# Two more VectorE instructions per rounding step in a two-layer macaron transformer on eight cores

## The reference

```python
x = x + 0.5 * ffn(layernorm(x), w1, conv_w, conv_b, w2)   # L0, call f0a
x = x + attn(layernorm(x))                                # L0
x = x + 0.5 * ffn(layernorm(x), ...)                      # L0, call f0b
x = x + 0.5 * ffn(layernorm(x), ...)                      # L1, call f1a
x = x + attn(layernorm(x))                                # L1
x = x + 0.5 * ffn(layernorm(x), ...)                      # L1, call f1b

def act_quant(x):
    scale = 127.0 / clip(max(abs(x), axis=-1), 1e-5)
    return clip(round(x * scale), -128, 127) / scale
def bit_linear(x, w):      # values of the forward pass
    return act_quant(x) @ weight_quant(w).T
def ffn(x, w1, conv_w, conv_b, w2):
    h = silu(depthwise_conv1d(bit_linear(x, w1), conv_w, conv_b))
    return bit_linear(h, w2)
```

## Time and profile before

| | us |
|---|---|
| median of the 2 runs shown | 11792.54 |
| fastest and slowest of them | 11703.24, 11881.84 |
| the profiled execution | 11800.77 |
| its span, from the first instruction of core 4 to the last | 11799.2 |
| spans of the 8 cores in it | 11674.3 to 11799.2 |

### The profile page before, as it was taken

One profiled execution on the slowest core, in us unless ns is written; L12 is line 12 of the kernel. 1 busy time (PEld: TensorE's weight loads), 2 busy tenths in 40 slices (PEclk: granted clock), 3 DMA queues, 4 the chain that ended last, 5 costly groups with the idle time before them and its releaser, 6 DMA issues.

```text
span 11799.2 us, 83085 instructions; the slowest of 8 cores (11674.3 to 11799.2 us)
## 1 busy us (share of the span) xinstructions
PE 8035.5 (68%) x27412; PEld 4436.9 (38%) x27412; DVE 4650.7 (39%) x5551; ACT 2367.6 (20%) x4432; POOL 1504.8 (13%) x1037
## 2 busy tenths in 40 slices
PE   0165768777899999846573155757799999883656
PEld 0022223232677677422221022223476777531222
DVE  4687741111111110148776587740101111017965
ACT  0221022222333333012100122021333333102200
POOL 0022510000000000002252012520000000000244
PEclk9677767776555555767776577868655555586877
DMA  6322210000000000001235412310000000000232
GB/s 219 109 80 96 74 36 27 32 32 27 29 11 11 22 11 1 15 14 79 96 75 181 140 64 97 75 42 26 24 4 8 4 4 4 15 14 25 96 94 85
DMA packets 134609, 619.99 MB, mean 53 GB/s; under 512 B 17193, under 2 KB 17737, under 8 KB 102250
## 3 DMA queue, kind: packets, MB, share of 16 engines
q1 hardware_dynamic: 70378, 253.67, 7.0%
q0 software_dynamic: 39616, 176.45, 4.6%
q10 hardware_dynamic: 24192, 184.56, 3.8%
HBM read 403.19 MB, written 209.85 MB: 52 GB/s over the span
## 4 chain that ended last, share of the span: by engine, by line
PE 49%; DVE 26%; DMA 10%; issue 6%; ACT 5%; POOL 2%; DVEq 1%; ACTq 0%; POOLq 0%; SPq 0%
PE pmLL L1420 7%; PE psS0L L1212 6%; PE psC0L L1198 5%; PE pmW L1328 4%; PE psC2L L1198 4%; PE psS2L L1212 4%; PE psC3L L1198 4%; PE psC1L L1198 4%; PE pmL1b L1647 1%; PE pmL1a L1583 1%; ACT L1230 1%; DVE sAf1a L666 1%; DMA g_wq<-wslP 1%; DVE sAf0a L666 1%; DVE sAf0b L666 1%
## 5 line engine op out<-in xcount | busy, mean ns | idle before, releaser
L1243 DVE TENSOR_TENSOR pr00L<-pr00L,maskt 128x128 f32<-128x128 f32 x128 | 37.4, 293 | 2825.0 <-ACT pr10L L1230 2825.0
L1328 PE MATMUL pmW<-woS,ctT 128*128 128x512 f32 x1024 | 523.9, 671 | 126.6 <-DVE ctT L1313 72.0
L411 ACT ACT_TABLE_LOAD x6 | 7.7, 1283 | 2959.9 <-DMA g_wq<-wslP 1260.4
L1230 ACT ACTIVATE pr00L<-psS0L,stats 128x256 f32<-128x256 f32 x576 | 272.5, 473 | 1034.9 <-PE psS1L L1212 1033.4
L1230 ACT ACTIVATE pr01L<-psS2L,stats 128x256 f32<-128x256 f32 x576 | 272.5, 473 | 1004.6 <-PE psS3L L1212 992.2
L725 POOL TENSOR_TENSOR zsq0f1b<-sZ0f1b 128x2048 f32<-128x2048 f32 x16 | 57.6, 3599 | 3159.0 <-DVE sAf1b L666 3013.4
L712 ACT ACT_TABLE_LOAD x124 | 159.1, 1283 | 1293.8 <-DVE sZ0f1b L694 167.0
L1420 PE MATMUL pmLL<-xlnT,wp0L 128*128 128x512 f32 x768 | 413.4, 710 | 7.6 <-DMA wp0L<-wq 7.6
L1420 PE MATMUL pmLL<-xlnT,wp1L 128*128 128x512 f32 x768 | 416.9, 715 | 0.0
L725 POOL TENSOR_TENSOR zsq0f0b<-sZ0f0b 128x2048 f32<-128x2048 f32 x16 | 57.6, 3599 | 2583.6 <-DVE sAf0b L666 2441.0
L1328 PEld LDWEIGHTS pmW<-woS,ctT 128*128 128x128 f32 x1024 | 214.9, 216 | 414.7 <-issue 414.7
(11 more groups left out here) (698 smaller groups left out, 20509.4 us busy)
## 6 DMA issues: line engine op xcount, KB each, us to landing
wbA<-w1t SPq DMA_DIRECT2D x8, 2048.0 KB
wbB<-w1t POOLq DMA_DIRECT2D x8, 2048.0 KB, 11.5
g_silu<-sZ0f0a ACTq DMA_DIRECT2D x16, 1024.0 KB, 3.9
g_silu<-sZ1f0a ACTq DMA_DIRECT2D x16, 1024.0 KB, 3.9
g_silu<-sZ0f0b ACTq DMA_DIRECT2D x16, 1024.0 KB, 4.0
g_silu<-sZ1f0b ACTq DMA_DIRECT2D x16, 1024.0 KB, 3.9
g_silu<-sZ0f1a ACTq DMA_DIRECT2D x16, 1024.0 KB, 4.0
g_silu<-sZ1f1a ACTq DMA_DIRECT2D x16, 1024.0 KB, 3.9
```

The costliest lines, as they stand in the source:

```text
L1230: T.inc(se.activation(pr[hd][v % 2][:], psS[2 * (v % 2) + hd][:, 0:256], AF.Exp, bias=stats[:, NEGM:NEGM + 1], scale=0.125), "se")
L1328: te.matmul(pm[:, nb * 512:(nb + 1) * 512], ctT[:, c * P:(c + 1) * P], woS[:, c * D + nb * 512:c * D + (nb + 1) * 512], start=(c == 0), st ...
```

## The change

In both roundings the constant ahead of the conversion to integer is lowered by 1, and the fraction left over, which then can be up to one larger, is compared with 2.0 as well as with 1.0; the two comparison results are added. In `vq` and in `vqb` this is one more comparison (a TENSOR_SCALAR, 128 x 1024 float32) into a new tile, and one more sum (a SCALAR_TENSOR_TENSOR, 128 x 1024 float32). The new comparison stands ahead of the old one. In `vqb` the tick `e_tick` stays on the old comparison. Each call gets two new SBUF tiles of 4 KB per partition, `xt2` (stage 2) and `e1b` (stage 4).

```diff
+RB2 = -1.0009765625
@@ vq, for each of 16 token tiles
-                        T.inc(ve.tensor_single_scalar(r0x[:], xt1[:], RB, ALU.add), "ve")
+                        T.inc(ve.tensor_single_scalar(r0x[:], xt1[:], RB2, ALU.add),
+                              "ve")
                         T.sw(ve, "ve")
                         T.inc(ve.tensor_tensor(xt0[:], xt1[:], r0x[:], ALU.subtract),
                               "ve")
                         T.sw(ve, "ve")
+                        T.inc(ve.tensor_single_scalar(xt2[:], xt0[:], 2.0, ALU.is_ge),
+                              "ve")
+                        T.sw(ve, "ve")
                         T.inc(ve.tensor_single_scalar(xt0[:], xt0[:], 1.0, ALU.is_ge),
                               "ve")
+                        T.sw(ve, "ve")
+                        T.inc(ve.scalar_tensor_tensor(xt0[:], xt2[:], 1.0, xt0[:],
+                                                      ALU.mult, ALU.add), "ve")
                         T.sw(ve, "ve")
@@ vqb, for each of 64 iterations
-                    T.inc(ve.tensor_single_scalar(r0b[:], Ub[:], 128.4990234375,
+                    T.inc(ve.tensor_single_scalar(r0b[:], Ub[:], 127.4990234375,
                                                   ALU.add), "ve")
                     T.sw(ve, "ve")
                     T.inc(ve.scalar_tensor_tensor(
                         buf[:], Ub[:], 128.5, r0b[:], ALU.add, ALU.subtract), "ve")
                     T.sw(ve, "ve")
+                    T.inc(ve.tensor_single_scalar(
+                        e1b[:], buf[:], 2.0, ALU.is_ge), "ve")
+                    T.sw(ve, "ve")
                     e_tick = T.inc(ve.tensor_single_scalar(
                         Ub[:], buf[:], 1.0, ALU.is_ge), "ve")
+                    T.sw(ve, "ve")
+                    T.inc(ve.scalar_tensor_tensor(
+                        Ub[:], e1b[:], 1.0, Ub[:], ALU.mult, ALU.add), "ve")
                     T.sw(ve, "ve")
```

More of the change, by code:

```diff
@@ L481, in ffn_call @@
                 xt1 = a0.enter_context(nc.sbuf_tensor(f"xt1{tag}", [P, D], F32))
+                xt2 = a0.enter_context(nc.sbuf_tensor(f"xt2{tag}", [P, D], F32))
                 r0x = a0.enter_context(nc.sbuf_tensor(f"r0x{tag}", [P, D], I32))
@@ L899, in ffn_call @@
                 r0b = b1.enter_context(nc.sbuf_tensor(f"r0b{tag}", [P, 1024], I32))
+                e1b = b1.enter_context(nc.sbuf_tensor(f"e1b{tag}", [P, 1024], F32))
                 qsl = [b1.enter_context(nc.sbuf_tensor(f"qsl{j}{tag}", [P, 1024], BF16))
```

## The result

| | before | after |
|---|---|---|
| median | 11854.59 us (10 runs) | 12444.99 us (11 runs) |
| lowest, highest | 11703.24, 11913.13 | 12342.35, 12503.44 |
| profiled execution | 11800.77 | 12413.86 |
| spans of its cores | 11674.3 to 11799.2 | 12246.3 to 12412.3 |

The change makes the kernel slower: ratio 1.0524, 95% interval 1.0467 to 1.0581, 590 us between the medians. The forecast was 12348 us with a range of 12120 to 12560. In some executions one die runs at a lower granted clock and takes longer; the ratios and their intervals leave those out, and the rows of e5 and e6, whose profiled executions were of this kind, are from a core of the other die.

What follows compares the result with a forecast made beforehand. The prediction took VectorE's serial chain to bound the input rounding and a loop through GpSimd's loads and products the second matmul; 136 + 411 = 547 us on the profiled 11800.8 gave 12348 us, range 12120 to 12560.

Steps and rivals of the forecast that it cites:

- Input rounding: Input rounding: two new VectorE instructions add 2.13 us per tile, covered by nothing; 16 tiles x 4 calls, 136 us.
- Second matmul: Second matmul: plain pairs of iterations grow by 3.52 us, block ends by less; 25.7 us per block, 16 blocks, 411 us.
- The loop load, comparison, product as the limit of before: Second matmul before: comparison, GpSimd's load issues, wait and product close on the pair's 12.75 us; VectorE idles 2.59.
- VectorE sets the pace after the change: Second matmul: VectorE's own 12.79 us per pair uses up its idle time; with stretches the pair becomes 16.26 us.
- Both pairs of products now cost VectorE time: Second matmul: without VectorE idle time, both pairs of GpSimd's products stretch its instructions, together 3.48 us per pair of iterations.
- The price of the odd products: Second matmul: GpSimd's products of odd iterations stretch VectorE's instructions by the usual 1.74 us; bounds nothing to 2.73.
- full blocking: Second matmul: one pair of products per pair of iterations costs VectorE 2.73, +120 us, 12468; both 12590; chance 0.17.
- the main case: Whole kernel: the summed growth of 547 us holds, time 12270 to 12420 us; chance 0.60.
- The ends of blocks: Second matmul: the first pair behind the correction grows by 2.5 us, the pair with the correction by 2.1.
- The rival that ended on the other side: Second matmul: VectorE displaces GpSimd undisturbed, so the stage barely grows; 11950 us, +1.3%, not slower by 2%; chance 0.05.
- The Trainium skill: Second matmul: strictly read, every pair of products costs VectorE 2.5 us; 17.8 per pair, about 180 us above the sum.
- Colder TensorE: Second matmul: longer idle puts matmuls ahead of the corrections at the lower clock level, +15 us, inside the range.

Runs made afterwards that it cites:

- e5: The changed kernel with GpSimd's products of the second matmul replaced by a plain copy on ScalarE (scale left out): 12034 us, second matmul 471 us shorter than in after.
- e6: The kernel before with GpSimd's products of the second matmul replaced by a plain copy on ScalarE (scale left out): 11415 us, ratio 0.9674.
- e1: The kernel before with the two new instructions only in the input rounding, second matmul unchanged: 12052 us, ratio 1.0196.
- f1: The kernel before with its four rounding instructions in either stage replaced by adding and subtracting a large constant: 11295 us, ratio 0.954.
- f2: f1 with the even loads of the second matmul from iteration 4 on issued by ScalarE in place of GpSimd: 10936 us, ratio 0.9231.
- e3: The kernel before with only the new comparison added in the second matmul, ahead of the tick, result unused: 12001 us, ratio 1.0115.
- e7: The changed kernel with the second load piece of each even iteration issued by SyncE in place of GpSimd: 12484 us, ratio 1.0545 to before.
- e4: The kernel before with only the new sum added in the second matmul, behind the tick: 12138 us, ratio 1.0295.

## Why the prediction was right, and where it was off

*Input rounding: right to the microsecond.* 136 forecast, 136 in after and in e1. Instructions, distances and the lack of cover were all as read.

*Second matmul: the mechanism right, the size 10% short.* 411 forecast, 456 measured. By its steps:

- The loop load, comparison, product as the limit of before: right (e6, -444 us without the product).
- VectorE sets the pace after the change, with no idle time: right. Its own 12.79 us per pair is what e5 shows.
- Both pairs of products now cost VectorE time: right, and without that there would be no growth. e5's second matmul is as short as that of before, 1756 against 1771 us, although it has all the new instructions; with the products on GpSimd it is 2227.
- The price of the odd products, 1.74 us: this term was mis-sized. They cost about 2.5 (3.17 and 3.29 against 0.69, 3.61 against 1.23). The prediction knew the long case from one row and argued it away: "at 1367.80 the short L943 began 0.03 ahead of GpSimd and the usual 1.74 followed, and the new neighbour would be such a short instruction too". That row is of an even pair of products, which GpSimd starts after a wait; the odd ones stand right behind its load issue, as the pair at 1342.93 beside the long sum of 3.96 did, and there a short neighbour is no protection (last section). The other argument, that 1225 is the median of L952, held for before only because most odd products began later than 0.4 us into it or into idle time. In after 913 of the 1024 odd pairs on the 8 cores stretched one VectorE instruction beyond 2.9 us, 795 of them the new comparison. The rival "full blocking" in its lighter form, one pair of products in two, given 0.17, is what happened, at 2.5 and not at its 2.73, and so the sign that the prediction had named for itself, a stretch that isn't near 1.74, was there for half of the products. The total came out nearer to the main case (547) than to this rival's 667 because of that smaller price, and because the edges below were smaller too. As mean over the four calls on the profiled cores a plain pair went from 12.86 to 16.93 us, +4.07 and not +3.52 (all pairs but the step across a correction and the pair behind it).
- The ends of blocks: the first pair behind the correction +2.9 (2.5 forecast). The step across the correction, from the start of the block's first rounding to the next, fell from 18.3 to 17.0 us in the mean; with the iteration ahead of it (6.1 to 8.1) that is +0.8, not +2.1. VectorE arrives later than most corrections and waits for few of them, so more of its rounding is covered than I took.
- By these and the last rounding's own +2.1, a call has 27 x 4.07 + 3 x (2.9 - 1.3) + 2.1 = 117 us more, four calls 467, against 468 measured on these two cores (2237 and 1769). The mean over the 8 cores is the 456.

*The rival that ended on the other side* needed VectorE to displace GpSimd without being displaced. The opposite holds in half of the cases: GpSimd's products kept their 2.50 and VectorE's instruction waited.

*The Trainium skill* ("SBUF — State Buffer", section "SBUF: two separate sides") has the loser of the shared ports fully blocked for the instruction of the other, and the ports held by whichever starts first. Read as the prediction read it, it gave 17.8 us per pair; the trace has 17.0 in the pair shown, 16.93 in the mean, between that reading and mine. The full block fits both patterns if each product counts as an instruction of its own. In the long one, the comparison was held until both products had ended (1246.86) and ended 0.55 later. In the usual one the two engines take turns, as the two products of 1251.02 show when they stand apart:

```profile
1251.02 1.78 POOL L940 TENSOR_TENSOR Ub0f0a<-rl0f0a,sb2f0a 128x512 f32<-128x512 f32 x1 [4.16 <-DVE qsl0f0a L968]
1252.76 2.24 POOL L940 TENSOR_TENSOR Ub0f0a<-rl0f0a,sb2f0a 128x512 f32<-128x512 f32 x1
```

r0b ends at 1251.67, the first product at 1252.80, L956 at 1253.88, the second product at 1255.00, the new comparison at 1255.55. That whoever starts first holds the ports doesn't agree with the long case: the comparison had started 0.12 us ahead of the products and lost nevertheless.

*Colder TensorE:* the granted clock in this stage was 0.79 to 0.82 in the four calls (0.80 before), while TensorE's busy time rose by 4 to 15 us per call. No cost of that can be seen: VectorE sets the pace, and the steps across the corrections, where it could count, got shorter.

## What to carry to other kernels

Idle time of an engine can be what keeps two engines apart. Before adding work to an engine with slack, look at what its neighbour on the same memory does during that slack: here 1.33 us more of VectorE per iteration cost 269 us of a possible 341, because GpSimd's products lost their undisturbed place. And price a stretch by the row whose situation is the same, not by its usual size: here by whether GpSimd's products stand right behind its own load issue, and how far into VectorE's instruction they begin. That decides between 1.7 and 2.5 us, or nothing for VectorE where idle time follows.

A rounding in four to six instructions is worth a second thought before its order is tuned: adding and subtracting one large constant does it in one instruction of 0.69 us (the median in f1; beside products it is longer, 1.46 and 1.02 in the rows of f2), and with the loads off the busy engine's order the kernel went to 0.923 of before.

## What the runs showed of the hardware that I had not expected

- A VectorE instruction already under way can be overtaken. The comparison started at 1244.24, with GpSimd's products starting at 1244.36, took 3.17 us while they took an undisturbed 2.50. In e3 a sum started at 1217.29, 0.03 ahead of GpSimd, took 3.61. But r0b, started 0.03 to 0.06 ahead of GpSimd (1250.98 and 1251.02 in after, 1252.26 and 1252.32 in e7), keeps 0.69, and then the products take 3.98 and VectorE's next two instructions 2.10 and 1.57. The costs are 2.4 to 2.75 for VectorE alone, or 1.74 for VectorE and 1.49 for GpSimd.
- What decides between them is in the traces of before, after, e1 to e4 and e7, over all 8 cores, if one sorts the pairs of products that begin during a rounding instruction. Of the pairs that GpSimd starts right behind its own load issue (within 0.1 us of its end) and less than 0.4 us after the start of VectorE's instruction, 3096 of 3097 stretched that instruction: comparisons, sums, remainders and, in e7, r0b 32 times. At 0.44 us or more, none of 1789 did. Of the pairs that GpSimd started after 0.24 us or more of idle time, 7194 of 7195 left it at its usual length (one added 1.1 us), at any distance, whatever the form. So it is not the form of the instruction, and the distance counts only behind a load issue. Two counter-examples to the form, r0b stretched in e7 (core 0) and a comparison spared in before (core 5):

```profile
1165.28 3.43 DVE L957 TENSOR_SCALAR r0bf0a<-Ub0f0a 128x1024 int32<-128x1024 f32 x1 [2.92 <-POOL Ub0f0a L944]
...
1165.06 0.58 POOL L55 DMA_DIRECT2D rl2f0a<-g_silu  x1
1165.66 2.49 POOL L944 TENSOR_TENSOR Ub1f0a<-rl1f0a,sb2f0a 128x512 f32<-128x512 f32 x2
```

```profile
1128.35 0.69 DVE L949 TENSOR_SCALAR Ub1f0a<-rl1f0a 128x1024 f32<-128x1024 f32 x1
...
1128.42 3.94 POOL L930 TENSOR_TENSOR Ub0f0a<-rl2f0a,sb2f0a 128x512 f32<-128x512 f32 x2 [2.38 <-DVE rl1f0a L946]
```

Why a load issue directly ahead makes this difference stays open, and no run changed it alone; the starts on GpSimd are as the profiler records them.
- VectorE's timing is otherwise exact: 12.79 us of 12 instructions came out as summed from two durations and one distance.
